# Row stage on row pairs: 1 KB runs in the stores, even and odd channels on the two halves of the partitions

## The reference

```python
# layer 0: a 3x3 filter per image and group of 4 channels, from the image's means
pooled = x.mean(axis=(2, 3))
lf = tanh(bn(pooled @ conv_w.T)).reshape(N, G, 1, 9, 1)
low = sum over 9 taps of patches(x) * lf
x = (low * (inside_all + 1) - inside_all * gap) * lamb_l + x * (lamb_h + 1)
# layer 1: Hartley transform, 20x20 modes mixed over channels, back, blurred
x_ht = dht_2d(x)
out_ht[:, :, :20, :20] = compl_mul2d(x_ht[:, :, :20, :20], w1)
y = dht_2d(out_ht) / (H * W)
y = gaussian_smoothing_4d(y)           # radius 4, over all four axes
return y * (abs(fftfreq(W)) <= 0.25)   # keeps some of the 128 image columns; the kernel computes 66
```

## Time and profile before

| | |
|---|---|
| median of 3 runs | 195.07 us (193.82 to 197.18) |
| profiled execution: own time | 193.97 us |
| its span, first to last instruction | 192.1 us |
| TensorE matmul busy | 169.2 us (88%), 1778 records |
| VectorE / ScalarE / GpSimd busy | 87.1 / 81.3 / 39.4 us |
| HBM read / written | 19.76 / 16.78 MB |
| granted TensorE clock over the span | 0.929 of full speed |

### The profile page before, as it was taken

One profiled execution on the slowest core, in us unless ns is written; L12 is line 12 of the kernel. 1 busy time (PEld: TensorE's weight loads), 2 busy tenths in 40 slices (PEclk: granted clock), 3 DMA queues, 4 the chain that ended last, 5 costly groups with the idle time before them and its releaser, 6 DMA issues.

```text
span 192.1 us, 4416 instructions
## 1 busy us (share of the span) xinstructions
PE 169.2 (88%) x1778; PEld 109.5 (57%) x1778; DVE 87.1 (45%) x189; ACT 81.3 (42%) x149; POOL 39.4 (21%) x21
## 2 busy tenths in 40 slices
PE   6589999999999999999999988999999999983500
PEld 3135656656564564656685778868767876761200
DVE  0002357198676868757456990223334333431200
ACT  2169774665565564564520091134343333331100
POOL 8992003008052160704204200000000000000000
PEclk9889999999999999999995599999999999999555
DMA  6999999999956366000000000008799999999997
GB/s 182 295 280 304 305 339 303 335 309 293 286 175 211 99 213 195 0 0 0 0 2 0 0 0 3 3 7 246 200 291 282 280 291 283 286 282 289 285 278 225
DMA packets 43795, 36.76 MB, mean 191 GB/s; under 512 B 692, under 2 KB 35676, under 8 KB 43780
## 3 DMA queue, kind: packets, MB, share of 16 engines
q1 hardware_dynamic: 43780, 36.54, 66.0%
HBM read 19.76 MB, written 16.78 MB: 190 GB/s over the span
## 4 chain that ended last, share of the span: by engine, by line
PE 71%; DMA 10%; SPq 4%; ACT 4%; DVE 3%; issue 2%; DVEq 0%
PE ps L381 15%; PE ps L413 12%; PE ps L550 11%; PE ps L391 9%; DMA x_ring<-x 5%; DMA out<-rows 5%; PE ps L509 5%; PE ps L529 4%; PE ps L400 4%; PE ps L401 4%; SPq L345 4%; PE ps L487 3%; ACT mixin L605 2%; PE ps L422 2%; ACT y_sb L617 1%
## 5 line engine op out<-in xcount | busy, mean ns | idle before, releaser
L381 PE MATMUL ps<-x_ring,k_wide 128*64 128x512 f32 x128 | 35.4, 632 | 3.6 <-DMA x_ring<-x 3.6
L550 PE MATMUL ps<-cols,k_wide 128*128 128x396 f32 (+2 forms) x96 | 31.7, 480 | 4.1 <-ACT rows L580 4.1
L617 ACT COPY y_sb<-ps 128x448 f32<-128x448 f32 x32 | 29.7, 933 | 9.9 <-PE ps L391 9.9
L612 ACT COPY freq<-ps 128x512 f32<-128x512 f32 x32 | 18.7, 586 | 29.7 <-PE ps L381 29.1
L391 PEld LDWEIGHTS ps<-k_wide,freq 128*128 128x128 f32 x128 | 13.7, 143 | 25.5 <-issue 24.4
L413 PEld LDWEIGHTS ps<-k_wide,y_sb 128*128 128x128 f32 x192 | 23.5, 194 | 7.3 <-ACT y_sb L617 4.2
L413 PE MATMUL ps<-k_wide,y_sb 128*128 128x44 f32 x192 | 24.8, 283 | 0.6 <-ACT y_sb L617 0.2
L550 PEld LDWEIGHTS ps<-cols,k_wide 128*128 128x128 f32 x96 | 17.8, 193 | 13.3 <-issue 5.3
L580 DVE COPY rows<-ps 128x396 f32<-128x396 f32 (+2 forms) x24 | 12.0, 502 | 22.6 <-PE ps L550 12.9
L580 ACT COPY rows<-ps 128x396 f32<-128x396 f32 (+1 forms) x24 | 11.1, 481 | 25.4 <-DMA out<-rows 13.5
L391 PE MATMUL ps<-k_wide,freq 128*128 128x128 f32 x128 | 21.5, 292 | 0.1
(11 more groups left out here) (66 smaller groups left out, 140.4 us busy)
## 6 DMA issues: line engine op xcount, KB each, us to landing
out<-rows SPq DMA_DIRECT2D x7, 1152.0 KB, 9.6
out<-rows SPq DMA_DIRECT2D x8, 896.0 KB, 8.7
w_sb<-mix_w SPq DMA_DIRECT2D x2, 960.0 KB, 10.1
out<-rows SPq DMA_DIRECT2D x3, 384.0 KB, 3.5
x_ring<-x SPq DMA_DIRECT2D x2, 512.0 KB, 5.3
k_wide<-wide SPq DMA_DIRECT2D x1, 533.0 KB, 7.8
x_ring<-x SPq DMA_DIRECT2D x15, 0.5 KB, 9.2
k_wide<-wide SPq DMA_DIRECT2D x1, 225.0 KB, 2.9
```

What stands on the lines that cost most here:

```text
L381: last = nc.tensor.matmul(ps[half * 64:half * 64 + 64, g % 2, :], const(O_LT, (1, 64)), x_ring[:, u, at:at + G1 // 2 * H], start=True, sto ...
L550: nc.tensor.matmul(ps[:, B_F[k % 3], 0:nt * NW], const(O_LH + s * H, (1, H)), cols[:, u, t:t + nt, :], start=True, stop=True).then_inc(f_d ...
L612: nc.scalar.copy(freq[:, g % 2, :], ps[:, g % 2, :]).then_inc(freq_out, 1)
L617: nc.scalar.copy(view(y_sb[:, u, 0, g * G1:g * G1 + 1], (1, G1 // 2), (G1 // 2, 2), (C, NP)), view(ps[:, 2 + g % 2, 0:1], (128, G1 // 2), ...
```

## The change

In the row stage a partition no longer holds one image row of all channels. It holds two neighbouring rows (2q and 2q+1) of all channels of one parity: partitions 0 to 63 the even channels, 64 to 127 the odd ones. For that the blurred channels are turned out in the order 0, 2, ..., 30, 1, 3, ..., 31 (`order` in the constants), the row constants are sorted by parity of the row, and a chunk is now (s, r, nt): channel pairs s, s+3, ..., rows of parity r. Each chunk takes two matmuls of 64 output rows, g = 0 for the even channels and g = 1 for the odd ones, into the two halves of one bank. The triples are 12, six for each parity. The layout of `rows` is [128, 2, 16, 2, 128]. Each image is stored in three transfers, one for each s, in which a run is two rows of one channel, 1 KB; store s waits for both of its chunks, 2s and 2s+1.

```diff
-TRIPLES = 11
+TRIPLES = 12
...
-        modes = sb("modes", [128, 2, (C + 1) * NF + 1])
+        modes = sb("modes", [128, 2, (C + 2) * NF + 1])
...
-        rows = sb("rows", [H, 2, C, H])
+        rows = sb("rows", [128, 2, C // 2, 2, H])
...
-        CHUNKS = [(s, t, (6 if t == 0 else (5 if s < 2 else 4))) for t in (0, 6) for s in range(3)]
-        FIRST = 18
-
-
-        PLACED = (1, 3, 3, 4, 5, 5)
-        ROUND = 5
+        CHUNKS = [(s, r, 6 if s == 0 else 5) for s in range(3) for r in range(2)]
+        PLACED = (1, 1, 2, 2, 3, 3)
+        ROUND = 3
...
-            for s in range(3):
-                sp.wait_ge(rows_dve if s == 1 else rows_act, PLACED[s])
-                sp.dma_start(out[0, s:FIRST:3, :, :].rearrange("c h w -> h c w"), rows[:, 0, s:FIRST:3, :]
-                             ).then_inc(out_done[0] if s == 2 else out_first, 16)
-            store(0, 0, FIRST, C, ROUND)
-            store(1, 1, 0, FIRST, PLACED[1])
-            store(1, 1, FIRST, C, ROUND)
+            by_pair = out.rearrange("n (k g) h w -> n k (g h w)", g=2).rearrange("n k (q e) -> n q k e", e=2 * H)
+
+            def store(n, u):
+                for s in range(3):
+                    sp.wait_ge(rows_act, n * ROUND + PLACED[2 * s])
+                    sp.wait_ge(rows_dve, n * ROUND + PLACED[2 * s])
+                    pairs = by_pair[bass.ds(n, 1), :, s:HC:3, :].rearrange("a q k e -> q (a k) e")
+                    sp.dma_start(pairs, rows[:, u, s:HC:3, :, :].rearrange("q k r w -> q k (r w)")
+                                 ).then_inc(out_done[u], 16)
...
+                    first = t // 6 * HC + t % 6 * 3
                     for half in (slice(0, 64), slice(64, 128)):
                         last = nc.tensor.matmul(ps[half, B_T + t // 6, (t % 6) * NW:(t % 6 + 1) * NW],
-                                                modes[half, u, 3 * t * NF:3 * t * NF + 64],
+                                                modes[half, u, first * NF:first * NF + 64],
...
                 if part == 0:
                     pe.wait_ge(cols_act, n + 1)
-                else:
                     pe.wait_ge(cols_dve, n + 1)
...
-                    nc.tensor.matmul(ps[:, B_F[k % 3], 0:nt * NW],
-                                     const(O_LH + s * H, (1, H)), cols[:, u, t:t + nt, :],
-                                     start=True, stop=True).then_inc(f_done, 1)
+                    for g in range(2):
+                        last = nc.tensor.matmul(ps[64 * g:64 * g + 64, B_F[k % 3], 0:nt * NW],
+                                                const(O_LH + s * H + r * H // 2, (1, H // 2)),
+                                                cols[:, u, 6 * g:6 * g + nt, :], start=True, stop=True)
+                    last.then_inc(f_done, 1)
...
-            s, t, nt = CHUNKS[k]
-            return copy(view(rows[:, u, 3 * t + s, 0:1], (3 * H, nt), (H - HALF, 2), (1, HALF)),
+            s, r, nt = CHUNKS[k]
+            return copy(view(rows[:, u, s, r, 0:1], (3 * 2 * H, nt), (H - HALF, 2), (1, HALF)),
```

More of the change, by code:

```diff
@@ L176, in constants @@
     wide = np.zeros((128, NC128), np.float32)
+    order = np.arange(C).reshape(C // 2, 2).T.reshape(-1)
     wide[:, O_LT:O_LT + NP] = lt
@@ L183, in constants @@
     wide[:, O_TW:O_LH] = tw
-    wide[:, O_LH:O_TURN] = lh.transpose(1, 0, 2).reshape(128, -1)
+    wide[:, O_LH:O_TURN] = lh.reshape(3, 128, H // 2, 2).transpose(1, 0, 3, 2).reshape(128, -1)
     for s in range(S):
@@ L187, in constants @@
             at = O_TURN + (s * Q + (q if s == 0 else Q - 1 - q)) * C
-            wide[q * C:(q + 1) * C, at:at + C] = blur_matrix(C).T
+            wide[q * C:(q + 1) * C, at:at + C] = blur_matrix(C).T[:, order]
     t, own = np.arange(KROWS) // J, np.kron(np.arange(KROWS) % J, 1)[:, None] == (np.arange(128) // C)[None]
@@ L281, in hartley_conv_kernel @@
         f_done, rows_act, rows_dve = map(sem, ("f_done", "rows_act", "rows_dve"))
-        out_first, out_done = sem("out_first"), [sem(f"out_done{i}") for i in range(2)]
+        out_done = [sem(f"out_done{i}") for i in range(2)]
         B_DATA, B_LF, B_COEF = 4, 5, 6
@@ L339, in _ @@
                     sp.dma_start(w_sb[:, cut, :], mix_w[:, cut, :]).then_inc(weights_in[n - 2], 16)
[L341 to L346, removed]
-            for s in range(3):
-                sp.wait_ge(rows_dve if s == 1 else rows_act, PLACED[s])
-                sp.dma_start(out[0, s:FIRST:3, :, :].rearrange("c h w -> h c w"), rows[:, 0, s:FIRST:3, :]
-                             ).then_inc(out_done[0] if s == 2 else out_first, 16)
-            store(0, 0, FIRST, C, ROUND)
-            store(1, 1, 0, FIRST, PLACED[1])
-            store(1, 1, FIRST, C, ROUND)
+            by_pair = out.rearrange("n (k g) h w -> n k (g h w)", g=2).rearrange("n k (q e) -> n q k e", e=2 * H)
[6 more added lines that the diff above has]
+                                 ).then_inc(out_done[u], 16)
+            for n in range(2):
+                store(n, n)
             with sp.Fori(1, N // 2) as it:
                 for u in range(2):
-                    store(it * 2 + u, u, 0, FIRST, PLACED[1])
-                    store(it * 2 + u, u, FIRST, C, ROUND)
-            sp.wait_ge(out_first, 32)
+                    store(it * 2 + u, u)
             for u in range(2):
-                sp.wait_ge(out_done[u], 32 * (N // 2))
+                sp.wait_ge(out_done[u], 48 * (N // 2))
         @block.tensor
@@ L687, in rows_step @@
                 if from_(it, 1) and chunks[0] < 3:
-                    act.wait_ge(out_done[u], it * 32)
+                    act.wait_ge(out_done[u], it * 48)
                 for k in chunks:
@@ L691, in rows_step @@
                     place_rows(nc.scalar.copy, k, u).then_inc(
-                        rows_act, PLACED[k] - (PLACED[k - 2] if k >= 2 else 0))
+                        rows_act, 1)
             def write_step(n, u, it):
@@ L704, in _ @@
                 write_step(n, n, 0)
-            act.wait_ge(out_first, 32)
             with act.Fori(1, N // 2 - 1) as it:
@@ L867, in rows_step @@
                 if from_(it, 1) and chunks[0] < 3:
-                    dve.wait_ge(out_done[u], it * 32)
+                    dve.wait_ge(out_done[u], it * 48)
                 for k in chunks:
@@ L871, in rows_step @@
                     place_rows(nc.vector.tensor_copy, k, u).then_inc(
-                        rows_dve, PLACED[k] - (PLACED[k - 2] if k >= 2 else 0))
+                        rows_dve, 1)
             def write_step(n, u, it):
@@ L884, in _ @@
                 write_step(n, n, 0)
-            dve.wait_ge(out_first, 32)
             with dve.Fori(1, N // 2 - 1) as it:
@@ L899, in _ @@
             nc.gpsimd.memset(modes[:, :, :], 0.0)
-            nc.gpsimd.memset(rows[:, :, :, :], 0.0).then_inc(zeroed, 1)
+            nc.gpsimd.memset(rows[:, :, :, :, :], 0.0).then_inc(zeroed, 1)
             pool.wait_ge(rest_in, 16)
```

## The result

The changed kernel takes 187.86 us (median, 186.96 to 188.25); the kernel before, on the same chips, 195.82. The ratio is 0.962, with a 95% interval from 0.952 to 0.972: faster. It compares the means of the fast runs, 187.73 us (all four) and 195.16 us (without one run of the kernel before, 197.18 us, which counts as slow). The profiled execution has a span of 186.4 us and a time of 188.25.

A forecast was written before the change was run, and what follows sets the result against it. Stores at 285 GB/s were taken to bound the write stage, TensorE being its floor. Data ready at 167.85 plus 16.0 us for 5.505 MB gives span 184.7, time 186.6, and 187.7 against the median; range 184.7 to 193.0.

The forecast's parts named there:

- What bounds it: Write stage: stores at 285 GB/s, 7.36 us an image, set the pace; TensorE's 6.43 us is the floor.
- The rate, 344 GB/s: Stores with 1 KB runs: 9.9 ns a run plus 0.0368 ns a byte give 344 GB/s, 6.10 us an image.
- The first rival: Store rate doesn't follow run length, staying at 285 to 305 GB/s: time 191.3 to 195.0; chance within a case given 0.19.
- Row products on halves, 3.75 us: TensorE's row products: twelve matmuls of 64 rows overlap in pairs, staying 3.75 us an image; serial 7.5, chance 0.02.
- +0.42 for changes of shape: Bad end for the row products: 1.97 ns a column in place of 1.78, so 4.17 us an image.
- Counting the weight loads at nothing: TensorE's 24 weight loads an image hide under matmuls; in the open 3.2 us an image, time 208.7, chance 0.02.
- The twelfth triple, +0.13 an image: TensorE's L529 grows from 22 to 24 matmuls, 1.43 to 1.56 us; an image's block becomes 6.56 us.
- The pattern of the stores: Rival: successive runs 384 KB apart in DRAM slow the stores; 2% slower needs 266 GB/s; chance 0.03.
- The sum: Write stage: block 6 at 165.59, queue empty at 167.85, then 5.505 MB in 16.0 us; span 184.7, forecast 187.7.
- data ends at 183.85: End of the write stage: the last 5.505 MB pass at 344 GB/s by 183.85, the span ends at 184.7.
- What would show it: Signs: 16,384 packets of 1 KB, windows near 340 GB/s, idle gaps, block pitch 6.56, TensorE done at about 176.5.
- No wait before the last two images: Sign in the write stage: ScalarE doesn't wait for `out<-rows` until the last two images.

The follow-up runs named there:

- serial halves: Against the changed kernel, each row product of a half writes all 128 output rows, so the two of a pair can't overlap: 209.8 us, one run.
- four-group kernel: Against the changed kernel, four image rows to a partition, four groups of 32 partitions, runs of 2 KB: 193.3 us, ratio to before 0.999.

## Why the prediction was right, point by point

- **What bounds it.** Right, as taking bytes away and taking run length away both showed. The stores were the limit at 285 GB/s, and TensorE's pitch was the floor to which a faster store could bring the stage: taking bytes away left the pitch at 6.49 us.
- **The rate, 344 GB/s.** Measured 341. Cost per run plus cost per byte, taken from loads, holds for stores up to 9 KB within 3% (packet times and rates). The line-rate rule of the Trainium skill ("DMA: Bandwidth & Descriptors", Specifications) says that 512 B are enough. The trace does not agree: 285 or 288 GB/s at 512 B, 341 or 344 at 1 KB, 416 at 7 to 9 KB. The first rival, a ceiling on written bytes, does not show up to that rate.
- **Row products on halves, 3.75 us.** Measured 3.70. The +0.42 for changes of shape, kept as the bad end, did not come: inside a block the pairs follow each other without a gap. Counting the weight loads at nothing was right too: with serial halves the block is 7.30 us, still without them in the open.
- **The twelfth triple, +0.13 an image.** Measured 1.55 against 1.43 for the piece, and taking it out again gave 0.12 back.
- **The pattern of the stores.** Runs 384 KB apart in a partition go as fast as those of the kernel before at the same run length (341 and 344 GB/s at 1 KB). This rival falls.
- **The sum.** Predicted: first row product 127.8, block 6 after 37.8, data 2.3 later, 16.0 for 5.505 MB, 0.8 to the end; 184.7. Measured: 128.5, 37.4, 2.6, 16.1, then 0.9 in which one engine alone still moves data, 0.9 to the end; 186.4. The mechanism and its terms hold; the step that was mis-sized is the end of the data, "data ends at 183.85". It took the 16 engines to end together, and it was short by the lag of one, about 0.9 us in this profile (0.5 in the second one). Another 0.7 us of the span is the start of the stage, which no part of the change moves. That 187.7 met the median of 187.86 more closely than this is luck: I added 1.1 us, by which the profiled execution of before lay below its median, and that of after lies 0.4 above its own.
- **What would show it.** 1 KB packets, about 340 GB/s, gaps of the DMA between blocks, TensorE done at 176.5 (177.1) all came. "No wait before the last two images" was too careful: there is none at all.

## What to carry to other kernels

Look at the length of the contiguous run in DRAM before the size of a transfer: a run costs about 8 ns of its engine beside 0.037 ns a byte, so 512 B loses almost a third of the long-run rate and 1 KB a fifth, and TensorE may give the longer run for nothing if its product splits into tiles that overlap. A faster transfer is worth only what it stood above the next bound, here TensorE's pitch, and the data of the last stretch, for which nothing is left to hide behind.

## What the runs showed of the hardware that was not expected

The supply of instructions is the likely limit of the four-group kernel. An unrolled TensorE stage with 272 instructions in 6.5 us runs beside full stores with small pauses only (0.2 us once, at 171.06; the larger one, 0.88 us, lies before the stage). With 416 it stops for up to 1.64 us at a time, once falls to half the clock for it, and the stage is 6.6 us longer than the changed kernel's; it runs without a long pause once the stores' bytes are cut to 3/8. The Trainium skill, "Runtime: NRT & Kernel Launch" (Instruction fetch mechanics), has this cost mostly hidden; if these pauses are that cost, it is not hidden in the trace of the four-group kernel. Splitting products into smaller tiles multiplies instructions, so it spends from this budget.
